# A two-layer attention and expert kernel: the second layer's output steps two slots later, its values stored by position and head, another order in the tail

## Chip, core and metric

One core of a Trainium2 chip. The metric is the device time of one execution in microseconds (us); lower is better. The kernel before was run three times, and once more with the profiler.

## The reference

`x` is 4 batches of 256 tokens with 128 features, `ctx` 4 batches of 512 tokens. Layer one is cross attention with 16 heads of 64 features, with rotated keys; layer two is attention *between the 16 heads of one token* (8 features each), followed by a mixture of 8 experts.

```python
# layer one: x + xattn(layernorm(x), ctx)
q = (lat @ Wq);  k, v = split(ctx @ Wkv);  k = apply_rope(k, cos, sin)
attn = softmax(clip(einsum('bhnd,bhsd->bhns', q, k) * scale, -11.0, 11.0))
x = x + (einsum('bhns,bhsd->bhnd', attn, v)) @ Wo + bo
# layer two: x + ffn(layernorm(x)), x being xl below
h = rmsnorm(x, gamma1)
q = (h @ Wq + bq).reshape(b, t, 16, 8)
k, v = split(((h @ Wdown + bdown) @ Wup + bup).reshape(b, t, 16, 16))
att = softmax(einsum('bthd,btgd->bthg', q, k) / sqrt(8))
x = x + einsum('bthg,btgd->bthd', att, v).reshape(b, t, 128) @ Wo + bo
h2 = rmsnorm(x, gamma2)
gate = softmax(h2 @ Wg + bg)
return x + einsum('btd,edf,bte->btf', h2, We, gate)
```

## The kernel before

Each engine has its own program, written out by hand, and semaphores tie them together. Layer one runs in 32 **slots**, one for each pair of heads: slot s holds batch s // 8 and pair s % 8. In slot s TensorE makes the keys of pair s + 3, the scores of s in two halves, the queries of s + 1, in even slots the row sums of s - 1, and the product of weights and values of s - 1. ScalarE takes the exponentials of the scores (L794), copies the high parts of queries (L777) and keys (L771) and the finished product (L802). GpSimd clips the exponentials (L1488) and adds the two halves of the rotated keys (L1481). VectorE multiplies keys with cosine and sine (L1048) and subtracts the high parts: the remainders of queries and keys (both L984). The scores of a slot need the remainders; the product needs the clip; the row sums too.

Between these stands the rest: the end of layer one and the whole of layer two, of the batch before. `POST_STEPS` (L62) places TensorE's steps: the key (n, "b") is position a, b or c in slot n counted from the batch's own first slot, so (8, "b") of the first batch is slot 16. The steps are norm0 to norm3 (the reciprocals of the row sums, spread over the heads, L665 and L666), out_proj, h_T, query_down, keyval2, then the second attention's output o_T (two transposes, L610) and out_proj2 (L705), then h2_T (transposes), gate (L713) and the expert products moe0 to moe3 (L718). All of these but those of the tail use one bank of PSUM, `side`, so each waits until the one before has been taken by ScalarE or VectorE. `OWN_STEPS` (L91) places the steps of the other engines in the same way: the words first, early, mid, late and end are places in VectorE's slot, in this order; a number is a place in GpSimd's (-1 before the first clip, 0 between the clips, 1 behind the second). VectorE's query and key remainders stand between early and mid. In mid the steps of an earlier batch stand before those of a later one, so a `reduce_1` at (8, "mid") stands before `reciprocals` (0, "mid") of the next batch; norm0 at (1, "a") waits for the latter.

The second attention of 128 tokens runs without TensorE: products of queries and keys into `prod` (L959), sums over 8 features (L1146), subtraction of the maximum (L1149, L1150), exponential (L888), weighted values (L967), sums over 16 heads (L1299) and the division (L1302). Tile 0 of a batch is VectorE's, for tile 1 GpSimd makes the products and VectorE the sums. Each product is done in two halves of 128 x 1024 elements. `kv2` holds keys and values as the weight `fwup` gives them: for each head g 8 key and 8 value features.

The last batch's layer two and the rest of the batch before it stand in the **tail**, from about 296 us: `last_batches` on VectorE (L1227) and GpSimd (L1496), `TAIL_STEPS` (L71) on TensorE over eight banks, and the list of steps behind ScalarE's loop.

## Time and profile before

| | us |
|---|---|
| median of 3 runs | 353.66 (352.28 to 353.86) |
| the profiled execution | 351.67 |
| its span | 349.9 |
| TensorE busy | 299.8 (86%) |
| VectorE busy | 252.7 (72%) |
| GpSimd busy | 206.8 (59%) |
| ScalarE busy | 155.4 (44%) |

Rows come from the profiled execution; times are counted from the start of its span. PE is TensorE's matmuls, PEld its weight loads, DVE VectorE, ACT ScalarE, POOL GpSimd. A group of matmuls of one line is shown as one row with its count. PEclk is the share of full clock that was granted: 1.00 is 2.4 GHz, 0.50 is 1.2 GHz.

### The profile page before, as it was taken

Reading aid. Unit: us, or ns where it says so; the run is one execution under the profiler, and the core shown is the slowest. Engines: PE = TensorE matmul, PEld = TensorE weight load, DVE = VectorE, ACT = ScalarE, POOL = GpSimd, SP = SyncE. Lnnn points to the kernel's source line nnn. Section 1 sums busy time; section 2 is a strip of 40 time slices with the busy share of each in tenths; the row PEclk is TensorE's granted clock in tenths of the full one; section 3 lists DMA queues with packets and bytes.
Section 4 is the critical chain, followed back from the end, with each engine's and each line's share of the span. In section 5 each row is a group of like instructions: output and inputs, shape, how many; then the busy total and the mean of one; then the engine's idle time right before and its main releaser. Section 6 shows DMA issues by size and latency. Waiting matters only on the chain.

```text
span 349.9 us, 6553 instructions
## 1 busy us (share of the span) xinstructions
PE 299.8 (86%) x2472; PEld 198.7 (57%) x2472; DVE 252.7 (72%) x470; ACT 155.4 (44%) x287; POOL 206.8 (59%) x206
## 2 busy tenths in 40 slices
PE   6768999999999999959999999949999999740862
PEld 6545666666686655636776556627776555620331
DVE  3957635435866489997938689996456697799977
ACT  3536454565434545533336475624425665020420
POOL 4527744544656486773755586982544788754661
PEclk9989999999999999998999999978999999995668
DMA  8843212211111111111101020111101000000001
GB/s 230 232 120 81 51 30 63 61 31 34 30 32 32 30 33 32 31 30 32 32 7 42 13 51 11 32 31 32 32 17 46 15 2 3 15 0 0 0 2 30
DMA packets 16318, 14.23 MB, mean 41 GB/s; under 512 B 4832, under 2 KB 11808, under 8 KB 16288
## 3 DMA queue, kind: packets, MB, share of 16 engines
q1 hardware_dynamic: 15232, 13.69, 15.0%
q8 instruction: 20, 0.33, 0.4%
q10 hardware_dynamic: 1056, 0.13, 0.2%
q14 instruction: 10, 0.08, 0.1%
HBM read 4.89 MB, written 0.52 MB: 15 GB/s over the span
## 4 chain that ended last, share of the span: by engine, by line
PE 61%; DVE 26%; ACT 6%; issue 3%; DMA 2%; POOL 1%; SPq 0%; ACTq 0%; DVEq 0%; POOLq 0%
PE pv L587 16%; PE sc L573 14%; PE sums L603 6%; PE pj_k L511 6%; ACT e L794 5%; DVE o L1299 5%; PE pj_k L513 3%; PE pj_k L512 3%; PE side L674 3%; DVE att L1146 2%; DVE o L1302 2%; DVE ks L984 2%; DVE prod L967 2%; DMA sin_in<-in_L_xattn_sin_dram 2%; PE side L718 2%
## 5 line engine op out<-in xcount | busy, mean ns | idle before, releaser
L1488 POOL TENSOR_SCALAR e<-e 128x1024 f32<-128x1024 f32 x64 | 68.9, 1077 | 75.9 <-ACT e L794 68.3
L794 ACT ACTIVATE e<-sc 128x1024 f32<-128x1024 f32 x64 | 65.7, 1027 | 80.8 <-PE sc L573 80.8
L573 PE MATMUL sc<-qs,ks 64*128 64x256 f32 x768 | 63.1, 297 | 6.7 <-ACT e L794 6.0
L573 PEld LDWEIGHTS sc<-qs,ks 64*128 64x128 f32 x768 | 50.1, 187 | 29.4 <-issue 17.6
L587 PE MATMUL pv<-e,v 128*64 128x256 f32 x512 | 65.5, 400 | 0.0
L1481 POOL TENSOR_TENSOR krot<-kcos,kswap 128x512 f32<-128x512 f32 x32 | 41.2, 1288 | 17.0 <-DMA kswap<-ksin 8.9
L587 PEld LDWEIGHTS pv<-e,v 128*64 128x64 f32 x512 | 35.2, 142 | 24.4 <-issue 8.9
L1048 DVE TENSOR_TENSOR ksin<-pj_k,sinT 128x512 f32<-128x512 f32 x32 | 22.1, 690 | 34.6 <-PE pj_k L513 30.7
L984 DVE TENSOR_TENSOR ks<-krot,ks 128x512 fp32r<-128x512 f32 x32 | 33.4, 1043 | 0.0
L802 ACT ACTIVATE u<-pv 128x256 f32<-128x256 f32 x32 | 12.3, 385 | 43.4 <-PE pv L587 43.4
L603 PE MATMUL sums<-e,sum_rows 128*32 128x256 f32 x512 | 30.9, 382 | 0.0
L967 POOL TENSOR_TENSOR prod<-att,kv 128x1024 f32<-128x1024 f32 x8 | 23.4, 2937 | 6.6 <-ACT att L888 6.2
L959 POOL TENSOR_TENSOR prod<-q,kv 128x1024 f32<-128x1024 f32 x8 | 19.5, 2448 | 5.6 <-DVE kv L1179 3.5
L771 ACT ACTIVATE ks<-krot 128x512 fp32r<-128x512 f32 x32 | 20.1, 627 | 4.9 <-POOL krot L1481 4.9
L1048 DVE TENSOR_TENSOR kcos<-pj_k,cosT 128x512 f32<-128x512 f32 x32 | 21.8, 681 | 0.0
L984 DVE TENSOR_TENSOR qs<-pj_k,qs 128x256 fp32r<-128x256 f32 x32 | 13.4, 420 | 11.3 <-ACT qs L777 11.3
L603 PEld LDWEIGHTS sums<-e,sum_rows 128*32 128x32 f32 x512 | 15.0, 109 | 11.0 <-POOL e L1488 0.8
L1299 DVE TENSOR_REDUCE o<-prod 128x64 f32<-128x1024 f32 x16 | 18.8, 1207 | 0.1
L511 PE MATMUL pj_k<-ctxT,wkA 128*128 128x512 f32 x32 | 16.0, 501 | 3.0 <-DVE kcos L1048 2.8
L786 ACT ACTIVATE v<-pj_k 128x512 f32<-128x512 f32 x28 | 16.6, 594 | 1.9 <-PE pj_k L513 1.6
L1530 POOL TENSOR_TENSOR moe<-moe 128x512 f32<-128x512 f32 (+2 forms) x18 | 15.4, 854 | 2.7 <-ACT moe L869 1.8
L967 DVE TENSOR_TENSOR prod<-own_bank,kv 128x1024 f32<-128x1024 f32 x8 | 15.4, 1932 | 0.1
(257 smaller groups left out, 535.4 us busy)
## 6 DMA issues: line engine op xcount, KB each, us to landing
kswap<-ksin SPq DMA_DIRECT2D x128, 64.0 KB, 2.0
ctx_in<-in_ctx_dram SPq DMA_DIRECT2D x4, 256.0 KB, 3.0
prod<-in_L_xattn_Wkv_dram SPq DMA_DIRECT2D x2, 512.0 KB, 6.1
x_in<-in_x_dram SPq DMA_DIRECT2D x1, 512.0 KB, 6.0
prod<-in_L_xattn_Wq_dram SPq DMA_DIRECT2D x1, 512.0 KB, 6.8
wo<-in_L_xattn_Wo_dram SPq DMA_DIRECT2D x1, 512.0 KB, 8.3
fwe<-in_L_ffn_We_dram SPq DMA_DIRECT2D x1, 512.0 KB, 4.8
out_dram<-x_in SPq DMA_DIRECT2D x3, 128.0 KB, 1.8
```

The lines of the kernel that those rows point to most:

```text
L511: nc.tensor.matmul(out_ap, w_hi, m_hi, start=True, stop=False)
L573: last = nc.tensor.matmul(sc[:, h, c * NT:(c + 1) * NT], ks[rows, j % 3, k_part, chunk], qs[rows, j % 2, q_part, :], start=(k_part + q_par ...
L587: last = nc.tensor.matmul(pv_bank[DH * h:DH * h + DH, 0:NT], v[:, c, col:col + DH], e[:, j % 3, h, c, :], start=(c == 0), stop=(c == SC - 1))
L603: last = nc.tensor.matmul(sum_bank[32 * g:32 * g + 32, 0:NT], w, e[:, (j - 1 + g // 2) % 3, g % 2, c, :], start=(p == 1 and c == 0), stop= ...
L771: nc.scalar.activation(ks[:, j % 3, 0, :], krot[:, j % 2, :], ACT.Copy).then_inc(s_khi, 1)
L794: nc.scalar.activation(e[:, j % 3, :, 2 * half:2 * half + 2, :].rearrange("p h c n -> p h (c n)"), sc[:, :, :], ACT.Exp, scale=SCALE).then ...
L967: return engine.tensor_tensor(prod[:, t, 1024 * hh:1024 * hh + 1024].rearrange("p (h d g) -> p h d g", h=G // 2, d=GD), weights(t)[:, 8 * ...
L984: return nc.vector.tensor_tensor(dst, whole, f(hi), ALU.subtract)
L1048: nc.vector.tensor_tensor(dst[:, j % 2, :], key_bank(j)[:, :], trig[:, :], ALU.mult).then_inc(s_kmul, 1)
L1299: return nc.vector.tensor_reduce(outputs(t)[:, 8 * hh:8 * hh + 8, :], pr, AX, ALU.add)
L1481: nc.gpsimd.tensor_tensor(krot[:, j % 2, :], kcos[:, j % 2, :], kswap[:, j % 2, :], ALU.add)\
L1488: nc.gpsimd.tensor_scalar(a, a, EXP_HIGH, EXP_LOW, ALU.min, ALU.max).then_inc(s_clip, 1)
```

## The change

Four things are changed.

1. o_T and out_proj2 of the first two batches move by two slots, h2_T, gate, moe0 and moe1 behind them, with the steps of VectorE, GpSimd and ScalarE that belong to them. The third batch's stand in the tail as before. `reduce_1` moves from early to mid, behind the remainders.
2. ScalarE writes a second copy of `fwup` and of its bias at the end of slot 6: first all keys by head, then the values by position and head. `kv2` is made from these, so the weighted values read 16 neighbouring elements for 16 heads.
3. In the tail VectorE makes the norms of `xl` between its two halves of products; ScalarE takes the exponential of tile 1 before h2_T.
4. In the tail GpSimd waits for both root norms (`t_hn2`) before the last expert sums.

```diff
@@ POST_STEPS
-    (3, "c"): "h_T", (4, "a"): "query_down", (4, "b"): "keyval2", (8, "b"): "o_T", (8, "c"): "out_proj2",
-    (10, "c"): "h2_T", (11, "a"): "gate", (13, "b"): "moe0", (13, "c"): "moe1", (15, "a"): "moe2",
+    (3, "c"): "h_T", (4, "a"): "query_down", (4, "b"): "keyval2", (10, "c"): "o_T", (11, "a"): "out_proj2",
+    (13, "a"): "h2_T", (13, "b"): "gate", (14, "b"): "moe0", (14, "c"): "moe1", (15, "a"): "moe2",
@@ OWN_STEPS
-    "reduce_1": [(8, "early")],
-    "root_norm": [(10, "first")],
-    "gate_exps": [(11, None)],
-    "gates": [(11, "late")],
+    "reduce_1": [(8, "mid")],
+    "root_norm": [(12, "mid")],
+    "gate_exps": [(13, None)],
+    "gates": [(14, "first")],
-    "mean_square": [(9, 1)],
-    "sum_experts_0": [(13, 1)],
-    "sum_experts_1": [(16, -1)],
+    "mean_square": [(11, 1)],
+    "sum_experts_0": [(15, 0)],
+    "sum_experts_1": [(16, 1)],
@@ TensorE, keyval2
+                    if b == 0:
+                        pe.wait_ge(s_kv_columns, 4)
-                                                fwup[:, :], start=True, stop=True)
+                                                fwkv[:, :], start=True, stop=True)
@@ ScalarE
+            def order_columns():
+                act.wait_ge(ld["ffn"], 16 * 6)
+                act.wait_ge(ld["bias"], 16 * 6)
+                for src, dst in ((fwup, fwkv), (fbup_r, fbkv)):
+                    of_heads = src[:, :].rearrange("p (g c) -> p g c", g=G)
+                    nc.scalar.activation(dst[:, 0:D].rearrange("p (g c) -> p g c", g=G), of_heads[:, :, 0:GD], ACT.Copy)\
+                        .then_inc(s_kv_columns, 1)
+                    nc.scalar.activation(dst[:, D:2 * D].rearrange("p (c g) -> p g c", g=G), of_heads[:, :, GD:2 * GD],
+                                         ACT.Copy).then_inc(s_kv_columns, 1)
@@ the slot loop
+                if slot == PAIRS - 2:
+                    order_columns()
@@ the tail
             weight_exps(LAST, 0)
+            weight_exps(LAST, 1)
             take("h2_T", before)
             gate_exps_of(before)
-            weight_exps(LAST, 1)
@@ products, weighted_values
-            k_v = kv2[:, t, :].rearrange("p (g c) -> p g c", g=G)[:, :, 0:GD]
+            k_v = kv2[:, t, 0:D].rearrange("p (g c) -> p g c", g=G)
-            v_v = kv2[:, t, :].rearrange("p (g c) -> p c g", g=G)[:, GD:2 * GD, :]
+            v_v = kv2[:, t, D:2 * D].rearrange("p (c g) -> p c g", g=G)
@@ VectorE, last_batches
                 products(nc.vector, 0, 0)
+                dve.wait_ge(s_x23, LAST - 1)
+                for t in range(TT):
+                    norm_tile(xl[:, LAST % 2, :, :], t, f_rstd, t_frstd).then_inc(t_xl, 1)
                 own(products(nc.vector, 0, 1))
                 query_tile(1)
                 keyval_tile(1)
-                dve.wait_ge(s_x23, LAST - 1)
-                for t in range(TT):
-                    norm_tile(xl[:, LAST % 2, :, :], t, f_rstd, t_frstd).then_inc(t_xl, 1)
@@ GpSimd, last_batches
+                pool.wait_ge(t_hn2, TT)
                 sum_experts(before, 1)
```

## Rows read from the trace of the kernel before

**Rows 1.** The page's busy times: engine, us, share of span, instructions.
```profile
PE 299.8 (86%) x2472; PEld 198.7 (57%) x2472; DVE 252.7 (72%) x470; ACT 155.4 (44%) x287; POOL 206.8 (59%) x206
```

**Rows 2.** Waits, whole span: engine, line, releaser: us, times, longest.
```profile
PE side L610 <- DVE o L1302: 8.5, 2, 4.7
```

**Rows 3.** Timeline of TensorE, 150 to 182: start, us, instruction, [idle before, releaser].
```profile
156.39 0.60 PE L610 MATMUL side<-ident,o 128*128 128x128 f32 x2 [3.75 <-DVE o L1302]
156.92 3.39 PE L587 MATMUL pv<-e,v 128*64 128x256 f32 x16
...
162.48 0.39 PE L665 MATMUL side<-recS,spread 128*128 128x256 f32 x1
...
165.93 1.95 PE L587 MATMUL pv<-e,v 128*64 128x256 f32 x16
```

**Rows 4.** Windows: stretch, length, TensorE busy (instructions), other engines, PEclk, DMA.
```profile
158.00:160.00 2.00, 2.00 (x14) 0.53 0.03 8
...
300.00:302.00 2.00, 2.00 (x20) 2.00 (x19) 1.67 (x3) 0.00 (x0) 2.00 (x1) 1.00 0.22 66
```

**Rows 5.** Timeline of TensorE, 198 to 242.
```profile
212.18 0.50 PE L511 MATMUL pj_k<-wvS,ctxT 128*128 128x512 f32 x1 [0.39 <-DVE qs L984]
...
233.42 0.66 PE L610 MATMUL side<-ident,o 128*128 128x128 f32 x2 [4.73 <-DVE o L1302]
...
240.21 0.39 PE L665 MATMUL side<-recS,spread 128*128 128x256 f32 x1
```

**Rows 6.** Lines 967 and 959: duration ns min/median/max, first and last start.
```profile
L967 DVE TENSOR_TENSOR prod<-own_bank,kv x8: 1869/1930/1989, 139.9 to 325.7; 128x1024 f32<-128x1024 f32 x8
L967 POOL TENSOR_TENSOR prod<-att,kv x8: 2847/2904/3269, 144.2 to 329.2; 128x1024 f32<-128x1024 f32 x8
...
L959 POOL TENSOR_TENSOR prod<-q,kv x8: 2322/2380/2713, 123.7 to 314.3; 128x1024 f32<-128x1024 f32 x8
L959 DVE TENSOR_TENSOR prod<-own_bank,kv x8: 1214/1220/1227, 123.8 to 310.0; 128x1024 f32<-128x1024 f32 x8
```

**Rows 7.** Instructions by line and shape: count, busy us, mean ns, idle before.
```profile
L869 ACT ACTIVATE moe<-side,gate 128x128 f32<-128x128 f32 x36 | 10.3, 378 | 2.1 <-PE side L718 2.0
```

**Rows 8.** Timeline of ScalarE, first exponential of slot 7.
```profile
75.24 1.02 ACT L794 ACTIVATE e<-sc 128x1024 f32<-128x1024 f32 x1 [1.41 <-PE sc L573]
```

**Rows 9.** Timeline of VectorE, slots 15 to 17 and slot 23.
```profile
149.00 2.73 DVE L1302 TENSOR_TENSOR o<-o,aden 128x128 f32<-128x128 f32 x1
...
157.10 1.75 DVE L1060 RECIPROCAL rec<-sums 128x256 f32<-128x256 f32 x1
...
159.49 0.42 DVE L984 TENSOR_TENSOR recS<-rec,recS 128x256 fp32r<-128x256 f32 x1
...
219.72 2.86 DVE L984 TENSOR_TENSOR ks<-krot,ks 128x512 fp32r<-128x512 f32 x1
```

**Rows 10.** Timeline of GpSimd, slot 15.
```profile
148.67 2.91 POOL L967 TENSOR_TENSOR prod<-att,kv 128x1024 f32<-128x1024 f32 x1
```

**Rows 11.** Timeline of GpSimd and of TensorE, slots 29 and 30.
```profile
281.97 1.05 POOL L1488 TENSOR_SCALAR e<-e 128x1024 f32<-128x1024 f32 x1
...
283.57 1.93 PE L603 MATMUL sums<-e,sum_rows 128*32 128x256 f32 x32
```

**Rows 12.** Timeline of VectorE, tail.
```profile
311.80 2.60 DVE L1167 TENSOR_SCALAR xl<-x_in,f_mv,f_rstd 128x128 f32<-128x128 f32 x2
...
325.62 0.17 DVE L1132 TENSOR_TENSOR gl<-gl,gmax 128x16 f32<-128x16 f32 x1
...
328.06 1.25 DVE L1140 TENSOR_TENSOR gate<-gl,gden 128x16 f32<-128x16 f32 x1
...
339.78 1.28 DVE L1194 TENSOR_SCALAR hn<-xl,rr 128x128 f32<-128x128 f32 x1 [0.44 <-POOL rr L1520]
```

**Rows 13.** Timeline of GpSimd, tail.
```profile
311.96 4.64 POOL L959 TENSOR_TENSOR prod<-q,kv 128x1024 f32<-128x1024 f32 x2 [3.46 <-DVE kv L1179]
```

**Rows 14.** Timeline of TensorE, norm0 of the last batch.
```profile
299.48 0.35 PE L665 MATMUL sc<-recS,spread 128*128 128x256 f32 x1 [1.52 <-DVE recS L984]
```

More of the change, by code:

```diff
@@ L258, in xattn_ffn @@
         fwup = sb("fwup", [L, 2 * D])
+        fwkv = sb("fwkv", [L, 2 * D])
+        fbkv = sb("fbkv", [128, 2 * D])
         fwo = sb("fwo", [128, D])
@@ L346, in xattn_ffn @@
         s_spread = sem("s_spread")
+        s_kv_columns = sem("s_kv_columns")
         s_cstat = sem("s_cstat")
@@ L1116, in take @@
                     nc.vector.tensor_tensor(kv2[:, :, :], side[:, :].rearrange("p (t n) -> p t n", t=TT),
-                                            twice(fbup_r), ALU.add).then_inc(free, 1)
+                                            twice(fbkv), ALU.add).then_inc(free, 1)
                     dve.wait_ge(*taken(name, b))
@@ L1178, in keyval_tile @@
                 dve.wait_ge(*made(f"keyval2/{t}", LAST))
-                nc.vector.tensor_tensor(kv2[:, t, :], side_banks[k][:, 0:2 * D], fbup_r[:, :], ALU.add)\
+                nc.vector.tensor_tensor(kv2[:, t, :], side_banks[k][:, 0:2 * D], fbkv[:, :], ALU.add)\
                     .then_inc(s_side_free[k], 1)
```

## The prediction

> **What bounds the kernel now.** I read the page's busy shares first, then the waits, then the timelines of TensorE, VectorE and GpSimd around the longest waits. TensorE is busy for 86% of the span [rows 1]; outside the tail the time is what TensorE works plus what it stands still. The waits name one standstill that is far longer than any other before the tail: the transposes of the second layer's output, o_T, wait 8.5 us in two goes for VectorE's last division [rows 2]. The timeline shows the first. The transposes begin at 156.39 after 3.75 us of idleness (the scores of slot 16 ended at 152.64), and behind them stand the values product of slot 15, 3.39 us long, and out_proj2; norm0 of slot 17 comes at 162.48 [rows 3]. The granted clock is 0.53 behind that wait (0.5 is the lower level, 1.2 GHz) [rows 4]; at the full clock the same 16 matmuls take 1.95 us [rows 3]. The second such place ends at 233.42 after 4.73 us, with norm0 at 240.21 [rows 5]. What ends last at both is VectorE's chain. In slots 12 to 16 it carries the second layer's sums, weighted values and divisions in front of what the next slot needs (query and key remainders, reciprocals of the row sums). In the tail, from 296 on, VectorE is the bound.
>
> **Part 1: values kept by position and head.** The weighted-value products read the values in steps of 16 elements before, side by side after. VectorE takes 1.93 us for one, GpSimd 2.90; the logits' products, of equal size and already with runs of eight, take 1.22 and 2.38 [rows 6]. The operands differ in little else, so I take 1.22 and 2.35 for the weighted values, with nothing saved as the other end. That is 0.7 us for each VectorE half, two halves a batch. The four ScalarE copies that prepare the weights stand at the end of slot 6. The nearest row, a gate-scaled copy of 128 elements, is 378 ns [rows 7], so they are at most 1.5 us. ScalarE stands idle for 1.41 us before the next exponential [rows 8]; I take 0, with 0.1 as the bound and 1.5 if that cover were gone. TensorE's new wait for them finds them made six slots earlier.
>
> The Trainium skill (GPSIMD Engine Reference, section "Performance pitfalls for Q7 kernels") gives some 50% more per element to reads with steps over 8 bytes; the trace shows 2.90 against 2.38, that is 22%. By the page GpSimd's weighted values would take 1.93 instead of 2.35, an estimate; the gates in part 5 (b) would then be ready 0.8 us earlier and the sum would be -5.7.
>
> **Part 2: o_T two slots later, first batch.** Now slots 15 to 17. The first half of the weighted values in slot 15 ends 0.7 us earlier (145.8 for 146.58), the reduction at 148.2. The division then meets GpSimd. In the trace it took 2.73 us, from 149.00 to 151.73, for 128 elements; GpSimd's product ran from 148.67 to 151.58 [rows 9, 10]. So a VectorE instruction with two operands in SBUF waits for the end of GpSimd's instruction. After the change that product runs from 148.2 to 150.5, and the division ends at 150.7.
> Behind the division come the weight sums 0.7, the key products 1.2, and now at once the query and key remainders 1.0 (to 153.7), then the reduction and division of the second half 2.6 (156.3), which were moved behind them, then the reciprocal part 2.8 (159.1; before, 157.10 to 159.91 [rows 9]). TensorE goes on at 152.64 with the values product 1.9 (clip done at 148.6), keys 0.9, scores 0.9, which brings it to 156.35, at full clock. There the standstill comes back, now in norm0, which needs the reciprocals: it waits 2.75 us, to 159.1. Before, norm0 was at 162.48: **-3.3**. o_T and out_proj2 (some 1.0 at full clock, estimated from the 0.60 of the transposes and as much again [rows 3]) now stand in slots 18 and 19, where h2_T and gate (some 1.0) leave: nothing in sum. VectorE's 0.9 us for out_proj2 also moves to slot 19, where it waits for keys. Ends: -5.3 if the division slips in ahead of GpSimd's product (the two are asked for within 0.1 us), -1.5 if neither product gets shorter and the clock falls.
>
> **Part 3: second batch.** The same place, slots 21 to 25, with two differences. Slot 21 gains gate, slot 22 gates and moe0, moe1: VectorE gets 1.1 us more ahead of the query remainder of slot 22, for which TensorE already waited at 212.18 [rows 5]. TensorE's 2.1 us of moe0 and moe1 stood before that wait and come after it. I follow both lines to slot 23: its scores start 1.7 us later. Part of this is swallowed by the wait in slot 25. Against it, the key remainder that took 2.86 us behind GpSimd's weighted values [rows 9] now stands behind the shorter expert sums that the change puts there. Reciprocals come at 236.5 for norm0, which was at 240.21: **-3.7**, ends -2 and -6.
>
> **Part 4: slots 29 to 32.** The moved work of the second batch lands where there are no keys and values left, so TensorE has nothing to hide a wait. Before, moe0 and moe1 filled slot 29 until 282; the row sums began at 283.57 and the clip they need ends at 283.02 [rows 11]. Without the two products TensorE is there at 282.0 and waits 1.0 us; then moe0, moe1 and moe2 go through one bank in slots 30 and 31, each waiting for ScalarE's four copies, which also stand ahead of the exponentials: 0.3 + 0.5 more. The last row sums begin 1.8 us later than before. At the reciprocals GpSimd's two weighted products now lie over VectorE's cast and subtraction, +0.3. **+2.1**, ends +0.5 and +4.
>
> **Part 5: tail.** (a) The two norms of xl took 2.60 us because GpSimd's products began 0.1 us after them [rows 12, 13]; moved ahead of these they take 0.6: 1.95 saved at 314.4. But the two square sums then come up at 316.05, and GpSimd is busy to 317.2: they end at 318.1 for 318.46; 0.35 is left. (b) The second exponential moves ahead of h2_T, so GpSimd's weighted values begin at 322.6 instead of 326.43, and the gates' product, 1.25 us at 328.06, is free again. But the second of them (324.9 to 327.2) now lies over the subtraction of the gate's maximum at 325.3, which is 0.17 us in the trace [rows 12]; VectorE resumes at 327.35 and the gates are ready at 329.2 for 329.31. (c) Expert sums start as VectorE asks for the division at 331.5, up to +0.8. (d) With GpSimd waiting for both root norms the last one takes 0.3 for 1.28 [rows 12], but the sums then hold up the gate 0.6 us later. I take **0** for the tail, ends -3.5 (none of these waits on GpSimd comes about) and +1.
> The Trainium skill (SBUF — State Buffer, section "SBUF: two separate sides") speaks against the tail's gain: the port pair that VectorE and GpSimd share is locked for a whole instruction, and the loser blocks fully. The 2.73 and 2.60 us above agree with it. Taken as a rule it gives the 0; were the port shared by halves, the tail would give about -3.
>
> **Sum.** -3.3 - 3.7 + 2.1 + 0 = -4.9 us. The profiled execution took 351.67 us (span 349.9 and 1.8 around it); it would be 346.8. The median of the three runs is 353.66, 2.0 above it, and by the same difference becomes **348.8**.
>
> **Rivals.** A: *the forecast*, the wait moves from o_T to norm0 and the clock stays up; chance 0.45, 346.5 to 350.5. B: *GpSimd's instructions lie well*: division ahead of GpSimd in one batch (-2), the tail keeps 2 to 3 us of its gain. For it: both are races of 0.1 to 0.4 us in my reckoning. Against it: GpSimd gets denser, so a chance request meets it more often. 342.5 to 346, middle 344.0; chance 0.27. C: *the clock falls all the same.* The wait at norm0 is 2.75 us, shorter than the 3.75 that was followed by a low clock [rows 3, 4], longer than the 1.52 us before the tail's norm0, behind which the clock is 1.00 [rows 4, 14]. Price: the product after it takes 3.39 for 1.95, about 1.5 us at each of two places. 351.8; chance 0.15. D: *the values' order saves nothing on either engine* (the step isn't the reason of the 1.93): VectorE is 0.7 to 1.4 us later at each of two places, so 351; chance 0.06. E: *slower*. Place: slots 22, 23 and 30, 31. The expert products share one bank, and each takes 1.05 us on TensorE and 1.14 on ScalarE before the next; two in one slot are 4.4 us if nothing else runs beside them. If over 3.5 us of it shows in each of the two stretches, the 7.0 us of parts 2 and 3 are gone; with all 4.4, and the rest of parts 4 and 5 as above, the end is at 355.8. Against it: the timeline has 1.9 us of values product between them. Chance 0.07.
>
> **Range and chances.** 342.8 to 352.4 leaves out E, a tenth of B and a third of C. Within 0.5% of 353.66 is 351.9 to 355.4; 0.5% is about what a measurement can tell here. A, B and D are below it, half of C is not: faster 0.84, same 0.11, slower 0.05.
>
> **What would show it.** Right: weighted values at 1.2 us on VectorE and 2.35 on GpSimd; no wait of the transposes on the division before the tail, but one of norm0 (spread products) on the recS subtraction, twice 2 to 3 us; the values product of slots 15 and 23 at 1.95 us and clock 1.0; row sums of slot 29 waiting for the clip; the xl norms at 0.6 us. Wrong: norm0 not waiting at all (then the gain is 2 to 5 us more), the clock at 0.5 behind it, the weighted values unchanged, or waits of exponentials and scores in slots 22 and 30 that add up to over 3 us each.

## The result, and the profile after

The changed kernel is slower. Its median is 357.13 us (356.25 to 357.91, 4 runs) against 353.65 for the kernel before on the same chip: ratio 1.0102, 95% interval 1.0074 to 1.0131. The forecast was 348.8 us with 352.4 as its upper end, so the sign was wrong too. The profiled execution took 356.25 us, its span is 354.4.

The first view is the page's busy times of the kernel after; the kernel before is in [rows 1].

```profile
PE 305.7 (86%) x2472; PEld 205.1 (58%) x2472; DVE 244.4 (69%) x470; ACT 156.6 (44%) x291; POOL 203.4 (57%) x206
```

VectorE has 8.3 us less work and GpSimd 3.4 less, but TensorE, with the same 2472 matmuls, is busy for 5.9 us more. It didn't get more work, it did it at a lower clock: the mean granted clock of the profiled execution is 0.930, for 0.943 before.

Part 1 of the change did what it says. Line 985 (967 before) holds the weighted values; the columns are least, median and longest duration in ns, and the first and last start. They answer to [rows 6].

```profile
L985 DVE TENSOR_TENSOR prod<-own_bank,kv x8: 1211/1216/1225, 141.2 to 332.5; 128x1024 f32<-128x1024 f32 x8
L985 POOL TENSOR_TENSOR prod<-att,kv x8: 2333/2364/2706, 145.5 to 330.2; 128x1024 f32<-128x1024 f32 x8
```

The waits of TensorE (total, times, longest) show that the 8.5 us of o_T [rows 2] are gone, and what stands in their place:

```profile
PE side L669 <- DVE recS L1002: 5.6, 2, 3.1
...
PE pj_k L515 <- DVE qs L1002: 3.2, 2, 2.7
...
PE sc L669 <- DVE recS L1002: 2.6, 1, 2.6
PE sums L607 <- POOL e L1506: 2.5, 3, 1.4
```

The timeline of TensorE shows five of these places. Line 669 is norm0, 515 the values of slot 22, 724 an expert product, 607 the row sums, 678 out_proj.

```profile
160.76 0.36 PE L669 MATMUL side<-recS,spread 128*128 128x256 f32 x1 [3.12 <-DVE recS L1002]
...
162.02 1.65 PE L577 MATMUL sc<-qs,ks 64*128 64x256 f32 x12
...
212.76 0.79 PE L515 MATMUL pj_k<-wvS,ctxT 128*128 128x512 f32 x1 [2.71 <-DVE qs L1002]
...
214.21 1.90 PE L724 MATMUL side<-fwe,h2T 128*128 128x512 f32 x2
...
238.92 0.36 PE L669 MATMUL side<-recS,spread 128*128 128x256 f32 x1 [2.47 <-DVE recS L1002]
...
297.35 1.93 PE L607 MATMUL sums<-e,sum_rows 128*32 128x256 f32 x32 [1.44 <-POOL e L1506]
...
303.73 0.36 PE L669 MATMUL sc<-recS,spread 128*128 128x256 f32 x1 [2.57 <-DVE recS L1002]
...
306.40 2.78 PE L678 MATMUL pv<-wo,on 128*128 128x128 f32 x16
```

The windows behind four of them: after the length come TensorE, its weight loads, VectorE, ScalarE and GpSimd, then the granted clock.

```profile
162.00:164.00 2.00, 2.00 (x14) 1.76 (x14) 1.43 (x3) 0.67 (x2) 0.00 (x0) 0.50 0.39 97
214.00:216.00 2.00, 2.00 (x3) 0.44 (x2) 1.78 (x3) 1.12 (x2) 1.27 (x1) 0.51 0.00 0
240.00:242.00 2.00, 2.00 (x13) 1.77 (x14) 1.50 (x3) 0.78 (x2) 2.00 (x2) 0.50 0.37 90
304.00:306.00 2.00, 2.00 (x15) 2.00 (x14) 1.43 (x3) 0.00 (x0) 1.09 (x3) 0.68 0.00 0
```

So in this profile every one of the four waits of 2.5 to 3.1 us on VectorE is followed by the lower level of the clock (that of 303.73 from 305 on: 0.68, then 0.50). Before, the two waits of o_T were [rows 3 to 5]; the two places at 212 and 303 are new. The drop doesn't come every time, as the section on the clock shows.

Where the span's 4.5 us come from. I lay the traces side by side by the start of the first exponential of each slot. The profile of before had a short start: in every other kernel of this study slot 1 is 0.4 to 2.2 us later, here 1.3, behind a low clock at the start (from 24 to 34 us) that lasts longer than in before and that none of the changes touches. So the columns count from slot 16 on. The last column compares with the kernel *values_and_tail* (below), which is the kernel after with the step tables of before: it is what the moved steps did, in one profile of each.

| at the start of | after minus before | after minus values_and_tail |
|---|---|---|
| slot 17 | -6.2 | -4.8 |
| slot 18 | -1.8 | -0.4 |
| slot 22 | -1.7 | -0.3 |
| slot 23 | +2.5 | +3.9 |
| slot 25 | -5.1 | -1.0 |
| slot 26 | -1.3 | +2.8 |
| slot 30 | -1.6 | +2.6 |
| slot 31 | +0.2 | +4.4 |
| last reciprocals done | +2.9 | +7.5 |
| end of span | +3.2 | +9.1 |

Slots 17 and 25 start early because their scores stand before norm0, which does the waiting now; the gain that stays is read a slot later. One profile is not the last word on such a row: gates_mid, sum_first and experts_behind_clip (below) have the steps of after up to slot 21, and their slot 18 starts 0.4 to 1.0 us later than that of after.

### The profile page after: what moved, and what is told of

The parts are those of the page before. It is cut to its first block, busy times and chain, and to the rows that moved or that the text cites. A ratio compares the mean times of both kernels' runs of the same rounds, so it can differ in the third digit from the quotient of the medians.

```text
span 354.4 us, 6558 instructions
## 1 busy us (share of the span) xinstructions
PE 305.7 (86%) x2472; PEld 205.1 (58%) x2472; DVE 244.4 (69%) x470; ACT 156.6 (44%) x291; POOL 203.4 (57%) x206
## 4 chain that ended last, share of the span: by engine, by line
PE 56%; DVE 26%; POOL 5%; ACT 5%; issue 4%; DMA 2%; SPq 0%; ACTq 0%; POOLq 0%; DVEq 0%
PE sc L577 13%; PE pv L591 11%; PE sums L607 6%; PE pj_k L515 6%; DVE o L1317 4%; PE pj_k L516 3%; PE pj_k L517 3%; ACT e L800 3%; PE side L678 3%; DVE ks L1002 2%; DVE att L1164 2%; DVE own_bank L1164 2%; POOL e L1506 2%; PE side L614 2%; DMA sin_in<-in_L_xattn_sin_dram 2%
## 5 line engine op out<-in xcount | busy, mean ns | idle before, releaser
L1506 POOL TENSOR_SCALAR e<-e 128x1024 f32<-128x1024 f32 x64 | 68.0, 1063 | 80.9 <-ACT e L800 72.8
L577 PE MATMUL sc<-qs,ks 64*128 64x256 f32 x768 | 65.3, 304 | 6.1 <-ACT e L800 5.0
L577 PEld LDWEIGHTS sc<-qs,ks 64*128 64x128 f32 x768 | 51.9, 194 | 28.7 <-issue 17.6
L591 PE MATMUL pv<-e,v 128*64 128x256 f32 x512 | 62.3, 385 | 0.0
L591 PEld LDWEIGHTS pv<-e,v 128*64 128x64 f32 x512 | 33.9, 136 | 22.9 <-issue 7.1
L1002 DVE TENSOR_TENSOR ks<-krot,ks 128x512 fp32r<-128x512 f32 x32 | 32.3, 1009 | 0.0
L985 POOL TENSOR_TENSOR prod<-att,kv 128x1024 f32<-128x1024 f32 x8 | 19.1, 2399 | 2.7 <-ACT att L894 2.4
L515 PE MATMUL pj_k<-wvS,ctxT 128*128 128x512 f32 x28 | 14.5, 519 | 3.2 <-DVE qs L1002 3.2
```

Source lines behind the costliest of these rows:

```text
L515: nc.tensor.matmul(out_ap, w_hi, m_hi, start=True, stop=False)
L577: last = nc.tensor.matmul(sc[:, h, c * NT:(c + 1) * NT], ks[rows, j % 3, k_part, chunk], qs[rows, j % 2, q_part, :], start=(k_part + q_par ...
L591: last = nc.tensor.matmul(pv_bank[DH * h:DH * h + DH, 0:NT], v[:, c, col:col + DH], e[:, j % 3, h, c, :], start=(c == 0), stop=(c == SC - 1))
L1002: return nc.vector.tensor_tensor(dst, whole, f(hi), ALU.subtract)
L1506: nc.gpsimd.tensor_scalar(a, a, EXP_HIGH, EXP_LOW, ALU.min, ALU.max).then_inc(s_clip, 1)
```

## The experiments

Each ran beside the kernel before on the same chip; the ratio is against it, and its medians lay between 353.0 and 353.65 us. A difference below between two changed kernels is one of medians from different rounds, so some tenths of it can be chance. "Tables" are POST_STEPS and OWN_STEPS.

| kernel | median us | ratio (95%) |
|---|---|---|
| after | 357.13 | 1.010 (1.007 to 1.013) |
| slots_alone | 362.78 | 1.026 (1.021 to 1.031) |
| values_alone | 348.01 | 0.986 (0.981 to 0.990) |
| tail_alone | 351.83 | 0.995 (0.993 to 0.998) |
| values_and_tail | 347.87 | 0.986 (0.982 to 0.990) |
| experts_late_alone | 362.34 | 1.026 (1.023 to 1.030) |
| reduce_late | 352.65 | 0.997 (0.993 to 1.000) |
| gates_mid | 355.68 | 1.009 (1.005 to 1.013) |
| experts_behind_clip | 356.52 | 1.011 (1.007 to 1.015) |
| sum_first | 354.07 | 1.001 (0.998 to 1.003) |
| three_mended | 353.60 | 0.999 (0.997 to 1.002) |
| filled_wait | 360.52 | 1.022 (1.018 to 1.026) |
| filled_short | 353.29 | 0.998 (0.996 to 1.001) |
| one_later | 350.03 | 0.991 (0.988 to 0.993) |
| behind_product | 350.21 | 0.991 (0.988 to 0.993) |
| product_filled | 351.99 | 0.997 (0.994 to 1.000) |
| values_tail_filled | 344.29 | 0.974 (0.971 to 0.977) |

### Which part costs

**slots_alone**: the kernel before with the tables of after and nothing else.

> The kernel before with the two tables of places of the changed kernel, and nothing else (values and tail as before). Theory S, the moved steps cost more than they free: slower than before, 355 to 358 us, with the scores of slot 23 at least 3 us late against those of slot 22, and the row sums of slot 31 waiting over 1 us for the clip behind the expert sums. Theory V, the moves gain and the new order of the values loses it (GpSimd's shorter products meet VectorE more often): 349 to 351 us.

Measured: 362.78 us, +9.8 us. **values_alone**: the kernel after with the tables and the tail of before.

> The kernel before with the values kept by position and head (the second copy of weight and bias, the four copies on ScalarE), the tables and the tail as before. Theory S: 1 to 3 us faster than before (350.5 to 352.5): each weighted product 0.7 us shorter on VectorE and 0.5 on GpSimd, partly lost in waits. Theory V: 1 us or more slower than before. In both the slots 0 and 1 show whether the 1.33 us that the changed kernel lost there belong to the change: if they do, they are here too; if they are chance, the shift at slot 1 is anything.

Measured: 348.01 us, -5.0 us. **tail_alone**: the kernel before with

```diff
             weight_exps(LAST, 0)
+            weight_exps(LAST, 1)
             take("h2_T", before)
             gate_exps_of(before)
-            weight_exps(LAST, 1)
```

and the two other changes of the tail.

> The kernel before with the changes of the tail alone: the norms of xl between the two products, the second exponential ahead of h2_T, GpSimd waiting for both root norms. From the ledger of the changed kernel's trace the tail behind the residual gained 1.1 us: 352.5. If a wait for GpSimd in the middle of its product eats the gain, as was predicted: 353.6. The full gain of 3 us (350.5) would mean that GpSimd's slower products, 2.9 us as before, leave the gate's subtraction free.

Measured: 351.83 us, -1.2 us by the medians and -1.6 by the ratio (interval 0.8 to 2.5). **values_and_tail**: both, with the tables of before.

> The changed kernel with the two tables of places of the kernel before: the values' order and the tail together, no step moved. If the parts add up (5.0 us and 1.2 us measured alone): 346 to 347. If GpSimd's shorter products take the tail's gain by meeting the gate's subtraction, as was predicted: 348.

Measured: 347.87 us. The moved steps cost 9.3 us on top of the other changes (357.13 less 347.87) and about as much without them (9.8). All that the change gained comes from the values' order and the tail; the moved steps, in which I had seen most of the gain, lose more than that.

### What in the moved steps costs: reduce_1, gates, expert sums

**reduce_late** (the kernel after with this edit alone):

```diff
-    "reduce_1": [(8, "mid")],
+    "reduce_1": [(8, "late")],
```

> The changed kernel with reduce_1 at (8, late) instead of (8, mid), so that the reciprocals of the row sums of the next batch stand before it. Theory S: norm0 of slots 17 and 25 no longer waits 3.12 and 2.47 us and the clock doesn't fall behind it (1.3 us each): 5 to 8 us faster than the changed kernel, 349 to 352. Rival: the wait only moves on to norm1 or to the next slot's remainders, because VectorE has the same work to do before slot 18: 355 or more.

Measured: 352.65 us, 4.5 us under after. The reduction now stands behind the next batch's reciprocals and norm0 hardly waits, but the next thing does: the values of slot 17, on the key products. This is that wait on TensorE's timeline, and the window behind it.

```profile
161.76 0.50 PE L515 MATMUL pj_k<-wvS,ctxT 128*128 128x512 f32 x1 [1.69 <-DVE kcos L1066]
...
164.00:166.00 2.00, 2.00 (x12) 1.16 (x10) 1.97 (x11) 0.00 (x0) 0.23 (x1) 0.50 0.13 33
```

VectorE's chain ends last there in any order; a wait moved from one consumer to the next is shortened, not gone, and this 1.69 us too was followed by the low clock. Of the 2.9 us that this profile is ahead of after at slot 31, 1.6 came in slot 22, which the edit doesn't touch: the wait there is 2.68 us as in after, but the clock stayed at 1.00 behind it.

**gates_mid** (`"gates": [(14, "mid")]` for `"first"`, so that the gates stand behind the remainders of slot 22):

> The changed kernel with gates at (14, mid) instead of (14, first): the gates' sum, reciprocal and product (0.15 + 0.17 + 0.81 us in slot 22) stand behind the query and key remainders. If they are what makes TensorE wait 2.71 us in slot 22: the wait falls to 1.5 us or less, the clock stays up behind it (another 1 us) and the scores of slot 23 come 2 us earlier: 354.5 to 355.5. If TensorE's late expert products are the cause (2.1 us that stood before the wait): less than 1 us, 356.5.

Measured: 355.68 us, 1.45 under after; the two intervals overlap, and its single executions lie between 353.84 and 356.88 us, so the gain isn't shown by the times. In the profile the wait in slot 22 is 1.96 us for 2.71 and slot 23 starts 0.65 us earlier in relation to slot 22; the clock fell behind it all the same. The gates' part of it is small in instructions but not in time. This is VectorE's timeline ahead of that wait in the kernel after:

```profile
205.42 0.17 DVE L1149 TENSOR_REDUCE gmax<-gl 128x2 f32<-128x16 f32 x1
205.63 1.26 DVE L1150 TENSOR_TENSOR gl<-gl,gmax 128x16 f32<-128x16 f32 x1
...
208.01 0.15 DVE L1156 TENSOR_REDUCE gden<-gl 128x2 f32<-128x16 f32 x1
208.20 0.17 DVE L1157 RECIPROCAL gden<-gden 128x2 f32<-128x2 f32 x1
208.40 0.81 DVE L1158 TENSOR_TENSOR gate<-gl,gden 128x16 f32<-128x16 f32 x1
```

The subtraction of 16 elements, 0.17 us when nothing is beside it [rows 12], took 1.26, to 206.89: GpSimd's addition of the key halves ran beside it, from 205.58 to 206.86. The gates' product took 0.81 in the same way. In gates_mid the three instructions of the gates are out of that wait, the subtraction is not, and 1.96 us are left.

**experts_behind_clip** (`"sum_experts_0": [(15, 1)]`):

> The changed kernel with sum_experts_0 at (15, 1) instead of (15, 0), behind the second clip of slot 31 instead of in front of it. If GpSimd's order makes the row sums of slot 31 wait 1.44 us: the wait goes, 1.4 us faster, and the product and the sums of slot 23 gain nothing: 355.7. If it goes lost in the tail (the reciprocals then meet GpSimd's weighted products one step further on): 357.

Measured: 356.52 us, 0.6 under after, which is inside both intervals. What the edit touches is mended: in TensorE's timeline of this kernel the last row sums come 1.2 us earlier than in after and no longer wait for the clip.

```profile
296.15 1.93 PE L607 MATMUL sums<-e,sum_rows 128*32 128x256 f32 x32
...
303.93 0.55 PE L669 MATMUL sc<-recS,spread 128*128 128x256 f32 x1 [3.98 <-DVE recS L1002]
```

But norm0 of the last batch then waits 3.98 us for 2.57. GpSimd's two weighted products, 4.66 us from 298.84, now lie over VectorE's cast and subtraction from their start to their end, and the gain is gone. **sum_first** moves the other sum instead:

```diff
-    "sum_experts_1": [(16, 1)],
+    "sum_experts_1": [(16, -1)],
```

> The changed kernel with sum_experts_1 back at (16, -1), so that in slot 32 GpSimd makes the expert sums (three additions of 1.3, 0.75 and 0.5 us) before the second half of the third batch's weighted values (2.3 us in one instruction). If it is GpSimd's long products over the cast and the subtraction of the last reciprocals that hold up norm0 of the tail (0.97 + 1.36 us for 0.65 + 0.63 before): these fall to 1.3 together, and with the wait of norm0 (2.57 us) under 2 us the clock stays up behind it: 1 to 2.4 us faster than the changed kernel, 354.7 to 356. If the order there makes no difference: 357.

Measured: 354.07 us, 3.1 under after. Here GpSimd's two weighted products don't follow each other over the last reciprocals. GpSimd and VectorE in the kernel after:

```profile
293.01 2.62 POOL L1550 TENSOR_TENSOR moe<-moe 128x512 f32<-128x512 f32 x3
295.71 0.45 POOL L1551 TENSOR_TENSOR x_in<-x_in,moe 128x128 f32<-128x128 f32 x1
296.25 1.04 POOL L1506 TENSOR_SCALAR e<-e 128x1024 f32<-128x1024 f32 x1
297.37 4.66 POOL L985 TENSOR_TENSOR prod<-att,kv 128x1024 f32<-128x1024 f32 x2
...
301.21 0.97 DVE L1080 CAST recS<-rec 128x256 fp32r<-128x256 f32 x1
302.22 1.36 DVE L1002 TENSOR_TENSOR recS<-rec,recS 128x256 fp32r<-128x256 f32 x1
```

and VectorE and TensorE in sum_first:

```profile
299.87 0.71 DVE L1080 CAST recS<-rec 128x256 fp32r<-128x256 f32 x1
300.61 0.63 DVE L1002 TENSOR_TENSOR recS<-rec,recS 128x256 fp32r<-128x256 f32 x1
...
301.38 0.36 PE L669 MATMUL sc<-recS,spread 128*128 128x256 f32 x1 [1.57 <-DVE recS L1002]
...
303.34 2.13 PE L678 MATMUL pv<-wo,on 128*128 128x128 f32 x16
```

One microsecond less in the cast and subtraction made the wait 1.57 us instead of 2.57. The clock stayed up behind it (out_proj 2.13 us for 2.78), which gave a second 1.4 us. Whether the shorter wait is the reason of that isn't shown: in the profiles of reduce_late, filled_short and gates_mid the same wait was 2.56 or 2.57 us long and the clock stayed at 1.00 too. And 1.1 us of this profile's lead was there at slot 31, ahead of the edit: a wait of 2.31 us in slot 25 without a low clock behind it. The last clip still stands behind the expert sums (296.25 above) in both kernels, and the row sums wait 1.44 us for it in both.

**three_mended** puts reduce_late, gates_mid and experts_behind_clip together.

> The changed kernel with reduce_1 at (8, late), gates at (14, mid) and the first expert sums at (15, 1) together. Alone against the changed kernel these gave -4.5, -1.4 and -0.6 us. If they add: 350.5; the moves then still cost over 2 us against the same kernel without them (347.9). If the second and third matter more once the first has taken the wait away (a wait further on then shows fully): 348 to 349.

Measured: 353.60 us. The single gains (4.5, 1.45 and 0.6) don't add up, and together they show no more than the first alone (352.65; the intervals overlap): cast and subtraction of the last reciprocals take 1.31 and 2.43 us under GpSimd's 4.67 us products, norm0 waits 3.98 us for them, and the clock falls behind that. Which instructions lie over each other decides here, besides their number.

**experts_late_alone** (tables of before, with only moe0 and moe1 at (14, "b") and (14, "c") and the sums at (15, 1) and (16, 1)):

> The kernel before, with only moe0 and moe1 moved to (14, b) and (14, c) and the expert sums with them ((15, 1) and (16, 1)); o_T, out_proj2, h2_T, gate, gates, the values and the tail as before. TensorE's 2.1 us of these products stood in slot 21 before its wait for the query remainder and now come after it. If that alone makes slot 23 late: its scores come 2 us later against those of slot 22 (they came 4.2 later with the whole change), 2 to 4 us slower than before, 355 to 357. If the lateness was the gates' doing: same as before, 353.5.

Measured: 362.34 us, +9.0 us, nearly as much as all moved steps (9.8). That the expert products are dear is seen best behind slot 29: slot 29 gains 0.7 us, slot 30 loses 2.3, the last reciprocals 3.7 (cast 1.64, subtraction 2.92 behind a GpSimd product), the clock behind them 1.7. Earlier the account isn't clean: slot 21 gains 1.5 and slot 22 loses 1.5, and 1.7 us crept in over steady slots in which no step had moved, at a granted clock of 0.95 where the other kernels have 1.00. That creep belongs to the profiled execution and not to the kernel: it took 364.2 us at a mean granted clock of 0.883, the other three 361.35 to 362.49 at 0.923 to 0.928. So the median's 9 us, and not less, are the cost of the products' move, with what the clock does behind it.

### What the clock behind a wait costs

**filled_short**: the kernel after with 11 matmuls of the identity with itself, 22 instructions in the trace, into the free bank ahead of norm0's wait in slots 17 and 25. (Later expectations call them transposes.)

```diff
+                    if name == "norm0" and 0 < b < LAST:
+                        for _ in range(11):
+                            nc.tensor.matmul(side[:, 0:128], ident[:, :], ident[:, :], start=True, stop=True)
                     if name == "norm0":
                         pe.wait_ge(s_recS, b + 1)
```

> The changed kernel with 11 matmuls of the identity (22 instructions, 2.6 us) in front of the wait of norm0 in slots 17 and 25 alone. In the run with twice as many, and with a useless group in slot 9 (4.7 us), slot 18 came 5.47 us late where 6.94 had been the delay before the place, although norm0 itself came 1.75 us late by the overshoot. If the clock is the price: it stays at 1.0 behind norm0, the scores there take 0.98 us instead of 1.65, 2 to 2.6 us faster than the changed kernel, 354.5 to 355. If not: 357.

Measured: 353.29 us, 3.8 under after, with 44 instructions more whose result nobody reads. The edit is the filler alone. TensorE's timeline, the window behind it, and the wait in slot 22 with its window:

```profile
158.33 2.72 PE L664 MATMUL side<-ident 128*128 128x128 f32 x22
161.90 0.39 PE L672 MATMUL side<-recS,spread 128*128 128x256 f32 x1 [0.85 <-DVE recS L1005]
...
162.00:164.00 2.00, 2.00 (x20) 1.73 (x21) 2.00 (x5) 0.44 (x2) 0.00 (x0) 1.00 0.13 33
...
212.49 0.50 PE L515 MATMUL pj_k<-wvS,ctxT 128*128 128x512 f32 x1 [2.69 <-DVE qs L1005]
...
214.00:216.00 2.00, 2.00 (x17) 1.06 (x16) 1.50 (x3) 1.63 (x6) 1.16 (x1) 1.00 0.00 0
```

The profile doesn't put all of the gain at the filled places. Against after, slot 18 starts 1.0 us earlier and slot 26 another 1.5: these 2.5 us are at the two filled places, although VectorE's own chain isn't shorter there. Another 1.6 came in slot 22 and some 1.4 behind the last norm0. Nothing was filled at these two, the waits (2.69 and 2.56 us) are as long as in after (2.71 and 2.57), and yet the clock stayed at 1.00. The profiled execution took 351.26 us; two others took 351.3 to 351.6 and seven 352.7 to 354.6. So the 3.8 us of the medians aren't the price of two waits alone, and whether the filler has a part in what happened at the other two is not shown.

The other profiles show the same. I take TensorE's waits between slot 1 and the last norm0 in all 18 kernels. The 23 of 2.71 to 5.84 us were all followed by the lower level, those of up to 1.68 us never. Of the 24 from 1.69 to 2.69 us, 14 were followed by it and 10 were not. The same wait at the same place is found on both sides: 2.57 us at the last norm0 with the low clock in after, without it in gates_mid; some 2.7 us in slot 22 with it in after and sum_first, without it in reduce_late and filled_wait. The single executions of one kernel differ along with it: those of sum_first lie between 351.22 us, at a mean granted clock of 0.955, and 356.72 at 0.923. So in this range the length of the wait alone doesn't decide, and what does is open; one profile can't tell what such a place costs on average. What the low clock costs when it comes is seen in slot 22: 1.6 us (slot 23 is 4.2 us later than in before with it, 2.6 without).

**filled_wait** had 22 such matmuls (44 instructions), and not where the expectation puts them: its condition is `b < LAST - 1`, so they stand in slots 9 and 17, and slot 25 has none.

> The changed kernel with 22 matmuls of the identity into the side bank in front of the wait of norm0 in slots 17 and 25 (about 2.4 us at full clock; nothing reads them). If the fall of the clock behind the wait costs 1.3 us at each place: the scores behind norm0 take 0.98 us instead of 1.65 and the kernel is 2 to 2.6 us faster, 354.5 to 355. If the fall has another reason: 357 or more.

Measured: 360.52 us, 3.4 *over* after. In slot 9 nothing waits and the filler is added nearly in full (5.18 us long, +4.7 there), and in slot 17 it lasts 5.18 us for a wait of 3.12: slot 18 starts 0.3 us later than in after, though the clock stays at 1.00. Where a filler is longer than the wait, the excess is a cost.

**values_tail_filled**: values_and_tail, with 8 matmuls of the identity (16 instructions) ahead of o_T's wait in slots 16 and 24, where the tables of before have it.

```diff
                 elif name == "o_T":
+                    if b < LAST - 1:
+                        for _ in range(8):
+                            nc.tensor.matmul(side[:, 0:128], ident[:, :], ident[:, :], start=True, stop=True)
                     from_tile(t_o2, s_o2)
```

> The values' order and the tail's changes with the tables of the kernel before, and 8 transposes of the identity (16 matmuls, some 2.0 us by the 2.72 us of 22 such) ahead of the transposes o_T of the first two batches, which wait 2.65 and 2.78 us for the division. The same kernel without them is at 347.87 us; its products behind the wait take 3.05 and 3.21 us for 1.95. Theory that the wait's price is partly the clock that falls behind it: the products take 1.95 us and the result is some 2.3 us lower, 345.5. Rival that the clock was not what the time hung on there (what comes next, the scores, waits for VectorE's remainders in any case): 347.5 to 348, with new waits of the scores.

Measured: 344.29 us, 3.6 under values_and_tail, and faster than both kernels of the case by 2.6 and 3.6%. TensorE's timeline first in values_and_tail, then with the filler:

```profile
157.20 0.66 PE L614 MATMUL side<-ident,o 128*128 128x128 f32 x2 [2.65 <-DVE o L1320]
157.79 3.05 PE L591 MATMUL pv<-e,v 128*64 128x256 f32 x16
```

```profile
156.02 0.44 PE L614 MATMUL side<-ident,o 128*128 128x128 f32 x2 [0.58 <-DVE o L1323]
156.39 1.95 PE L591 MATMUL pv<-e,v 128*64 128x256 f32 x16
```

The division ends at the same time in relation to slot 16 in both (within 0.1 us); the rest of the wait is filled, and only the clock behind it differs. By the profiles the first place gives 1.4 us, the second 1.6; the 3.6 of the medians is some tenths more. These two waits, 2.65 and 2.78 us, were followed by the low level in both profiles without the filler (values_alone and values_and_tail), and all four executions with it lie between 344.0 and 344.8 us. This pair is the best evidence on the clock in the study.

### Other places for o_T

**one_later** (values_and_tail with o_T at (8, "c"), out_proj2 (9, "a"), norms and out_proj a position later, h2_T (11, "a"), gate (12, "c"), gates (13, "first")):

> The values' order and the tail, with another placement: o_T at (8, c), behind the product of values, out_proj2 at (9, a), the norms and out_proj one position later, h2_T at (11, a), gate at (12, c), gates at (13, first), and moe0 and moe1 where they were before. The 2.8 us that TensorE waits in o_T at slots 16 and 24 are covered by 1.9 us of the product of values, the clock stays up, and no expert product stands behind the wait of slot 22: 2 to 4 us faster than the values' order and the tail alone (347.9), 344 to 346. If norm0 waits for the reciprocals instead, as in the changed kernel: 347 to 348.

Measured: 350.03 us, 2.2 over values_and_tail. It gains at slots 17 and 25 and gives back 2.1 us in slot 21 and 2.4 in slot 29. No wait of this profile before the tail is followed by a low clock (the longest is 1.68 us): what it loses is lost by the placement of the steps.

**behind_product** (values_and_tail with o_T at (8, "c"), behind the values product, and out_proj2 in a new position between keys and scores of slot 17):

> The values' order and the tail, all places as before but two: o_T behind the product of values (8, c), and out_proj2 in slot 9 between the keys and the scores. No expert or gate step moves. TensorE then does the product's 1.9 us while VectorE reduces and divides, waits 0.9 us in o_T instead of 2.8, and the clock doesn't fall: 2 us or more at each of slots 16 and 24, 343 to 345 against the 347.9 without it. If the wait turns up at norm0 in full (the reciprocals come 3.9 us behind the division): 347 to 348.

Measured: 350.21 us, 2.3 over values_and_tail. TensorE's timeline:

```profile
157.40 0.41 PE L614 MATMUL side<-ident,o 128*128 128x128 f32 x2 [0.76 <-DVE o L1321]
...
162.52 0.58 PE L669 MATMUL side<-recS,spread 128*128 128x256 f32 x1 [2.55 <-DVE xl L1141]
...
164.31 1.65 PE L577 MATMUL sc<-qs,ks 64*128 64x256 f32 x12
```

The product does hide o_T's wait (0.76 us for 2.65). But norm0 now waits for something else than the reciprocals: for the one bank `side`, which VectorE empties with the addition to `xl` only after the key products of the slot. The wait is as long as the old one and the low clock comes with it.

**product_filled** is behind_product with 8 matmuls of the identity ahead of norm0.

> The kernel with o_T behind the values product and out_proj2 between keys and scores (350.21 us), and 8 such transposes ahead of norm0 in slots 17 and 25, which waits 2.55 us there and is followed by a clock of 0.50 for some 7 us. In that kernel the wait lies in front of norm0 instead of o_T, and the low clock costs 5.4 us from slot 17 to slot 18. Theory that nearly all of that is the clock: slot 18 starts 2.5 to 4 us earlier in relation to slot 17, likewise in slot 26, and the result is 344.5 to 347. Rival that VectorE is what ends last there: not under 349.

Measured: 351.99 us, 1.8 over behind_product. My filler stood in the wrong place:

```profile
160.74 3.41 PE L664 MATMUL side<-ident 128*128 128x128 f32 x16 [2.55 <-DVE xl L1144]
```

It writes to `side`, so it waits for the same bank; it filled nothing and came on top, at the low clock. This run therefore says nothing on the clock's price there.

## Why the prediction was wrong

**Part 1, values' order: right in size, wrong in its worth.** 1.22 and 2.36 us stood in the forecast as 1.22 and 2.35. I let it count only within the waits of parts 2 and 3. Alone it is worth 5.0 us, where two VectorE halves of 0.7 us at two places make 2.8: they stand on the chain that ends last at o_T, and GpSimd's halves end earlier too, as does each wait that they lengthen. How the rest divides, no run tells. ScalarE's four copies cost nothing, as forecast: from slot 1 to slot 16 the two traces keep their distance of 1.3 us within 0.05. On the Trainium skill's rule (GPSIMD Engine Reference, "Performance pitfalls for Q7 kernels"), some 50% more for reads with wide steps: the reading in steps took 2.90 us against 2.36, 23% more, so the trace and not the page gave the size.

**Part 2, first batch: -3.3 forecast, -1.8 measured.** The wait was forecast at the right place: norm0 at 160.76 with a wait of 3.12 us (2.75 forecast), which from slot 16 on is 3.05 us earlier than before. The division met GpSimd's product as forecast and took

```profile
149.54 2.40 DVE L1320 TENSOR_TENSOR o<-o,aden 128x128 f32<-128x128 f32 x1
```

The step that failed is "at full clock": rival C came true, 1.3 us, against the 1.5 that it had there. I had placed 2.75 us between the 3.75 that was followed by a low clock and the 1.52 that wasn't, and took the side of 1.52 without a row for it. The runs put a forecast of 2.75 us at the edge of where the clock always fell (2.71 and up), and the wait that came was 3.12. In all four profiles with these steps and the new values' order (after, gates_mid, sum_first, experts_behind_clip) it was 3.12 us or more and the clock fell; slot 18 was then 0.8 to 1.8 us earlier than before, so the 1.8 of this profile is the best of four.

**Part 3, second batch: -3.7 forecast, +0.4 measured.** Two steps failed. "Its scores start 1.7 us later" is 4.2 in the trace. It is the sum of three. The query remainder is 0.9 us later (1.1 forecast). moe0 and moe1, which stood ahead of the wait, stand behind it and add 1.7 of their 2.1 us. The low clock behind that wait adds 1.6 more: in reduce_late and filled_short, where the clock stayed up behind the same wait, the 4.2 are 2.6. The first two were in my text; a wait that VectorE ends isn't shortened by taking TensorE's work away from in front of it, so they add up to 2.6 and not to 1.7. From slot 23 to norm0 the rest went as forecast: -5.1 us by the trace, -5.4 by my numbers (-3.7 less 1.7). Behind norm0 the clock takes 1.3 again. That was chance in part: this wait is 2.47 us here, and behind 2.48 and 2.31 us at the same place in gates_mid and sum_first the clock stayed up.

**Part 4, slots 29 to 32: +2.1 forecast, +5.6 measured.** The last row sums are 3.2 us later, for 1.8: moved sums of the experts stand on GpSimd ahead of the last clip, 3.1 us, and the row sums wait 1.44 us for it. The diff has this (`sum_experts_0` at (15, 0)) and I counted TensorE and ScalarE of that move, not GpSimd's queue: that is the step that failed here. The cast and the subtraction cost 1.05 more (0.3 forecast), and the wait of 2.57 us that results brought the clock down once more, 1.4 (not so in gates_mid, reduce_late and filled_short, behind the same wait). That place had 1.52 us before [rows 14] and a full clock; nothing in my forecast asked what a longer wait would do to it.

**Part 5, tail: 0 forecast, -1.1 measured;** tail_alone gives 1.2 less by the medians, 1.6 by the ratio (0.8 to 2.5). The norms of xl take 0.59 us, as forecast, and the square sums behind them pay, as forecast; and the gate's subtraction lies under a product of GpSimd, again as forecast. What was mis-sized are (b) and (c): in relation to the first transpose of the tail the gates are ready 0.6 us earlier (0.1 forecast), and the division, which I let lose up to 0.8 to the expert sums, takes 0.29 us for 0.63 before. VectorE's timeline:

```profile
315.62 0.59 DVE L1185 TENSOR_SCALAR xl<-x_in,f_mv,f_rstd 128x128 f32<-128x128 f32 x2
...
321.71 1.30 DVE L1101 CUSTOM_DVE_ANT_0 hn<-xl 128x128 f32<-128x128 f32 x1
...
330.63 1.95 DVE L1150 TENSOR_TENSOR gl<-gl,gmax 128x16 f32<-128x16 f32 x1
```

The Trainium skill's rule (SBUF — State Buffer, "SBUF: two separate sides"), that the loser of the shared port pair blocks for the whole instruction, agrees with these: 1.30 for 0.29, 1.95 for 0.17.

**Rivals.** B and D fell (the tail kept 1 to 2 us; the values' order saved all that it could). C came true at norm0 twice, and at two places more that it didn't name; at all but the first of these four the clock stayed up in other profiles behind a wait within 0.2 us of it. E had the right side and one right place, the row of the expert products, but the wrong mechanism: it asked for the products to wait for each other in one bank, and that wait is 0.33 us in slot 30. The price came from where these products stood in relation to a wait, from GpSimd's sums, and from the clock.

**The sum by the trace:** -1.8 + 0.4 + 5.6 - 1.1 = +3.2 us from slot 16 on, and 1.3 for the short start that the profile of before happened to have: 4.5, the difference of the spans. The medians differ by 3.5. values_alone's profile shows 3.7 us of its 5.0 from slot 16 on, since behind its first wait the low clock lasted some 3 us longer than in before; values_and_tail, which does the same up to the tail, is 1.5 us ahead of it there. So how long the low level lasts differs from profile to profile as well, and what the four low stretches of after cost on average stays open. The chances of the prediction are slightly off by its own rule, too: A, B, D and half of C make 0.855, not 0.84.

## What to carry to other kernels

Price a wait of the matrix engine by its length and by what is behind it at half clock, with a chance: here a wait of over 2.7 us always cost it, one of 1.7 to 2.7 us in 14 cases of 24. One profile shows one outcome, so compare the granted clock behind the same wait in several profiles before an edit gets the credit. Count a moved step on every queue that it has an instruction on, and say on which side of an existing wait it lands: work taken from before a wait and put behind it costs most of its length (1.7 of 2.1 us here). Where a wait can't be removed, matmuls on idle operands into a free bank, shorter than the wait, gave 1.0 to 1.6 us a place here by the profiles.

## What the runs showed that I had not expected

- The clock behind a wait: a wait of the same length at the same place was followed by the low level in one profile and not in the next (1.69 to 2.69 us: 14 of 24). When it came it cost 1.0 to 2.0 us at most places, once 3 (values_alone).
- Reading one operand in steps of 16 elements costs VectorE 58% (1.93 us against 1.22 for 1024 elements) and GpSimd 23% (2.90 against 2.36).
- Two-operand instructions of 16 elements on VectorE took up to 1.95 us for 0.17 under GpSimd's products. Mending GpSimd's order at one place made such a meeting at another: all three kernels with the first expert sums at (15, 1) (experts_behind_clip, three_mended, experts_late_alone) have the last cast and subtraction under GpSimd's products.
